# An attention tower on one core: score banks fixed by the parity of the key chunk, a ring of three banks for the row maxima, and more negated maxima written ahead of the scores

## The reference, cut to what matters

```
h = relu(grouped causal conv(emb_table[x]))          # x: (2, 1024) ids, h: (2, 1024, 128), fp32
h = h + Attn(layernorm(h))                           # 8 heads of 64, Wq, Wk, Wv: 512 x 128, Wo: 128 x 512
h = h + FFN(layernorm(h))                            # 8 experts, each on fixed 128-token blocks, exact gelu
Attn(x):  q, k, v = x Wq', x Wk', x Wv'              # per head
          softmax(q k' / 8) v, heads joined, times Wo', plus x
FFN(x):   n = layernorm(x) * ln_g + ln_b;  t = n attn_w' + attn_b + x
          y = fc2(gelu(fc1(t)));  gelu(y next_w' + next_b)
```

## Time and profile before

| what | value |
|---|---|
| median of 3 runs | 402.38 us (402.29 to 402.70) |
| profiled execution, its time | 402.42 us |
| its span in the trace | 400.6 us |
| TensorE clock granted | 0.999 of full speed |
| busy share PE, ACT, DVE, POOL | 97%, 64%, 57%, 73% |

### The profile page before, as it was taken

One profiled execution on the slowest core, in us unless ns is written; L12 is line 12 of the kernel. 1 busy time (PEld: TensorE's weight loads), 2 busy tenths in 40 slices (PEclk: granted clock), 3 DMA queues, 4 the chain that ended last, 5 costly groups with the idle time before them and its releaser, 6 DMA issues.

```text
span 400.6 us, 6437 instructions
## 1 busy us (share of the span) xinstructions
PE 390.3 (97%) x2486; PEld 233.1 (58%) x2486; DVE 227.0 (57%) x310; ACT 254.6 (64%) x347; POOL 292.9 (73%) x145
## 2 busy tenths in 40 slices
PE   8989999999999999999999999999999989999996
PEld 7755554644555455455544644555449445489995
DVE  6998656565666556565656475656562800664322
ACT  3666568586767657666757575767662795436763
POOL 3170399969899899989898999899898588800021
PEclk9999999999999999999999999999999999999999
DMA  4001020101210211132022401240124015000001
GB/s 145 5 0 53 2 53 3 53 2 55 55 53 3 80 29 53 12 97 55 1 54 56 152 8 55 54 157 3 58 52 159 0 56 157 0 2 16 13 28 52
DMA packets 28226, 19.43 MB, mean 49 GB/s; under 512 B 21248, under 2 KB 23680, under 8 KB 28196
## 3 DMA queue, kind: packets, MB, share of 16 engines
q1 hardware_dynamic: 27620, 18.05, 16.7%
q10 hardware_dynamic: 576, 0.98, 0.7%
HBM read 17.72 MB, written 1.17 MB: 47 GB/s over the span
## 4 chain that ended last, share of the span: by engine, by line
PE 91%; DVE 6%; ACT 2%; issue 1%; ACTq 0%
PE acc_o L600 29%; PE slot L588 26%; PE slot L526 10%; PE slot L514 5%; PE slot L535 4%; PE acc_o L656 4%; PE slot L645 4%; PE acc_o L490 2%; PE slot L611 2%; DVE half_maxes L992 1%; PE slot L465 1%; PE slot L551 1%; PE slot L553 1%; PE acc_o L664 1%; PE slot L439 1%; ACT normed L811 1%
## 5 line engine op out<-in xcount | busy, mean ns | idle before, releaser
L992 DVE TENSOR_REDUCE half_maxes<-slot 128x2 f32<-128x1024 f32 x128 | 156.3, 1225 | 96.6 <-PE slot L526 96.4
L778 ACT ACTIVATE probs<-slot 128x1024 f32<-128x1024 f32 x128 | 124.6, 1024 | 82.1 <-PE slot L588 82.1
L600 PE MATMUL acc_o<-probs,v_all 128*64 128x512 f32 x512 | 123.7, 604 | 0.0
L1191 POOL TENSOR_TENSOR sums<-sums,probs 128x1024 f32<-128x1024 f32 x31 | 73.9, 2383 | 2.4 <-ACT probs L778 2.4
L1191 POOL TENSOR_TENSOR odd_sum<-odd_sum,probs 128x1024 f32<-128x1024 f32 x31 | 74.3, 2397 | 0.0
L1191 POOL TENSOR_TENSOR sums<-probs 128x1024 f32<-128x1024 f32 x16 | 37.8, 2365 | 42.6 <-ACT probs L778 42.6
L600 PEld LDWEIGHTS acc_o<-probs,v_all 128*64 128x64 f32 x512 | 31.2, 136 | 58.8 <-issue 39.7
L526 PE MATMUL slot<-k_round,q_round 64*128 64x512 f32 x256 | 56.8, 446 | 1.7 <-DVE half_maxes L992 1.4
L526 PEld LDWEIGHTS slot<-k_round,q_round 64*128 64x128 f32 x256 | 23.6, 183 | 57.2 <-issue 46.3
L588 PE MATMUL slot<-q_round,k_round 64*128 64x512 f32 x256 | 51.6, 399 | 1.1 <-DVE k_rest L987 0.6
L588 PE MATMUL slot<-q_round,k_rest 64*128 64x512 f32 x256 | 50.4, 389 | 0.0
(11 more groups left out here) (124 smaller groups left out, 418.0 us busy)
## 6 DMA issues: line engine op xcount, KB each, us to landing
max_plane<-rows_scratch SPq DMA_DIRECT2D x16, 512.0 KB, 3.7
inv_sb<-inv_scratch SPq DMA_DIRECT2D x14, 256.0 KB, 3.9
max_rows_of<-maxes SPq DMA_DIRECT2D x128, 0.5 KB, 2.0
v_all<-in_fc SPq DMA_DIRECT2D x4, 512.0 KB, 5.7
fc_late<-in_fc SPq DMA_DIRECT2D x4, 512.0 KB, 5.7
out_h<-probs SPq DMA_DIRECT2D x8, 128.0 KB, 1.8
v_all<-in_w ACTq DMA_DIRECT2D x3, 256.0 KB, 3.6
woT<-in_wo SPq DMA_DIRECT2D x1, 256.0 KB, 3.6
```

What stands on the lines that cost most here:

```text
L600: last = pe.matmul(acc_o[head_rows(h), cols], v_all[:, s, kc, head_rows(h)], probs[unit(s, kc, half) % TILES][:, h, :], start=(kc == 0), s ...
L778: act.activation(probs[u % TILES][:, :, :].rearrange("p h n -> p (h n)"), slot[:, :], ACT.Exp, scale=SCALE).then_inc(exped, 1)
L992: dve.reduce_max(half_maxes[:, :, qc, keys], slot[:, :].rearrange("p (h n) -> p h n", h=2), AX.X).then_inc(maxed, 1)
L1191: pool.tensor_tensor(chain[:, :, :], first[:, :, :], probs[kc][:, :, :], ALU.add).then_inc(own, 1)
```

## The change

- **Banks by kind.** A unit with an even `kc`, `k` and `wo` always take banks 0 and 1, one with an odd `kc` and `q` banks 2 and 3. Banks 4, 5, 6 are a ring: each max, `nt` and `xa` takes the next two of it, `den` and `last den` the next one. Bank 7 alone is the output of `pv` for both halves, so the first `pv` of a half waits for the copy `o` of the half before; step 7's half 0 is now copied too. The tail uses a spare ring bank and bank 7 in place of `acc_o`.
- **Waits by bank.** An item waits for the last holder of each of its banks (`holders`). A max in the steps is reduced in two instructions, one for each bank, each of which frees its bank.
- **More filled units.** 96 of 128 are in `FILLED`: 13 of 16 in steps 1 to 6 (not `kc` 0, 1, 3 of half 0), 10 in step 0 and 8 in step 7. Of them 45 (even `kc`, except `kc` 2 of half 0) are halved: item `share`, which stands between the two units of the part before, makes ScalarE write one bank and VectorE the other. The other 51 are written whole by ScalarE behind the second unit.
- **Maxima.** Parts 1 and 2 of step 0 take three each, so all later parts are 14 ahead rather than 12, and step 7 has maxima in part 0 alone.

```diff
-PREFILLED = (2, 4, 6)
-UNFILLED = ((0, 2, 0), (STEPS - 1, 4, 0), (STEPS - 1, 4, 1))
+LATE_PLANES = [(s, kc, 0) for s in range(STEPS) for kc in (0, 1)]
+BEHIND_K, BEHIND_Q = [(s, 2, 0) for s in range(STEPS)], [(s, 3, 0) for s in range(STEPS)]
+UNFILLED = LATE_PLANES + BEHIND_Q + [(0, 2, 0), (0, 0, 1), (0, 1, 1), (STEPS - 1, 2, 0), (STEPS - 1, 4, 0), (STEPS - 1, 5, 0), (STEPS - 1, 0, 1), (STEPS - 1, 1, 1)]
+ALL_UNITS = [(s, kc, half) for s in range(STEPS) for half in range(2) for kc in range(KCH)]
+FILLED = [u for u in ALL_UNITS if u not in UNFILLED]
+HALVED = [u for u in FILLED if u[1] % 2 == 0 and u not in BEHIND_K]
...
+def maxes_before(turn):
+
+    return AHEAD + 2 * turn + min(2, max(0, turn - 1))
...
-    maxes = [("max", *m) for m in MAXES[AHEAD + 2 * (s * PARTS + part):][:2]]
+    turn = s * PARTS + part
+    maxes = [("max", *m) for m in MAXES[maxes_before(turn):maxes_before(turn + 1)]]
     items = maxes[:1]
-    items += [("exp", *u) for u in units_of(s, part)] + maxes[1:]
+    first, second = [("exp", *u) for u in units_of(s, part)]
+    following = units_of(s, part + 1) if part + 1 < PARTS else []
+    items += [first] + [("share", *u) for u in following if u in HALVED] + [second] + maxes[1:]
     beside = beside_values(s, part)
     items += beside
-    if part % 4 < 3:
-        items.append(("fill", *units_of(s, part + 1)[0]))
+    items += [("fill", *u) for u in following if u in FILLED and u not in HALVED]
...
-        items += [("o", s, 0)] * (s + 1 < STEPS) + [("inv", s - 1)] * (s > 0)
+        items += [("o", s, 0)] + [("inv", s - 1)] * (s > 0)
...
+OUT_BANK, EVEN_PAIR, ODD_PAIR, RING = 7, (0, 1), (2, 3), (4, 5, 6)
...
+def step_pairs(items):
+
+    pairs, turn = [], 0
+    for item in items:
+        if item[0] == "exp":
+            pairs.append(ODD_PAIR if item[2] % 2 else EVEN_PAIR)
+        elif item[0] in ("k", "wo"):
+            pairs.append(EVEN_PAIR)
+        elif item[0] == "q":
+            pairs.append(ODD_PAIR)
+        else:
+            count = 1 if item[0] in ("den", "last den") else 2
+            pairs.append(ring_banks(turn, count))
+            turn += count
+    return pairs, turn
...
+def holders(n):
+
+    found = []
+    for bank in PAIRS_OF[n]:
+        held = [m for m in range(n) if bank in PAIRS_OF[m]]
+        if held:
+            found.append((held[-1], PAIRS_OF[held[-1]].index(bank)))
+    return found
...
             def weigh_values(item):
 
                 _, s, kc, half = item
-                cols = slice(half * BANK, (half + 1) * BANK)
                 pe.wait_ge(exped, unit(s, kc, half) + 1)
-                if kc == 0 and s > 0:
-                    pe.wait_ge(o_copied, 2 * s - 1 + half)
+                if kc == 0 and s + half > 0:
+                    pe.wait_ge(o_copied, 2 * s + half)
...
+                        for m, k in holders(n):
+                            pe.wait_ge(*release(ALL_ITEMS[m], k))
```

More of the change, by code:

```diff
@@ L120, in step_items @@
     return items
-NO_SLOT = ("join", "hidden", "pv", "o", "inv", "norms", "fill")
+NO_SLOT = ("join", "hidden", "pv", "o", "inv", "norms", "fill", "share")
 def numbered(items, first):
@@ L141, with ring_banks, filled_up_to @@
 ALL_ITEMS = PROLOGUE + [i for items_of_step in STEP_ITEMS for i in items_of_step if i[0] not in NO_SLOT]
-FIRST_SLOT, LATE_SLOT, SUMS_SLOT = ((FIRST[-1] - 3 + i) % SLOTS for i in range(3))
+OUT_BANK, EVEN_PAIR, ODD_PAIR, RING = 7, (0, 1), (2, 3), (4, 5, 6)
+def ring_banks(start, count):
+    return tuple(RING[(start + i) % len(RING)] for i in range(count))
+def step_pairs(items):
[12 more added lines that the diff above has]
+    return pairs, turn
+STEP_PAIRS, TURN = step_pairs(ALL_ITEMS[len(PROLOGUE):])
+PAIRS_OF = [(2 * (n % SLOTS), 2 * (n % SLOTS) + 1) for n in range(len(PROLOGUE))] + STEP_PAIRS
+SUMS_PAIR, FIRST_PAIR, LATE_PAIR, SPARE_BANK = ring_banks(TURN - 1, 2), EVEN_PAIR, ODD_PAIR, ring_banks(TURN + 1, 1)[0]
+def holders(n):
[5 more added lines that the diff above has]
+    return found
 def unit(s, kc, half):
     return s * UNITS + half * KCH + kc
[L150 to L157, removed]
+def filled_up_to(turn, units):
+    return len([u for u in units if 2 * u[0] + u[2] <= turn])
 def tile_added(s, kc):
@@ L610, in denominators @@
                         quad = 32 * (2 * h + half)
-                        last = pe.matmul(slot[quad:quad + 32, 0:BANK], ones[:, 0:32], sums[s % 2][half][:, h, :], start=True, stop=True)
+                        last = pe.matmul(slot[quad:quad + 32, 0, :], ones[:, 0:32], sums[s % 2][half][:, h, :], start=True, stop=True)
                 last.then_inc(filled, 1)
@@ L623, in last_denominators @@
                     for i, part in enumerate(parts):
-                        last = pe.matmul(slot[head_rows(h), 0:BANK], ones[:, :], part[:, h, :],
+                        last = pe.matmul(slot[head_rows(h), 0, :], ones[:, :], part[:, h, :],
                                          start=(i == 0), stop=(i == len(parts) - 1))
@@ L856, in _ @@
                 for item, n in numbered(STEP_ITEMS[s], FIRST[s]):
-                    if item[0] == "fill" and item[1:] in FILLED:
+                    if item[0] in ("fill", "share") and item[1:] in FILLED:
                         fill(item)
@@ L986, in dve_item @@
                     dve.wait_ge(rounded, 2 * v + (1 if kind == "k" else 2))
-                    dve.tensor_tensor(rest[v % 2][:, :], slot[:, :], whole[v % 2][:, :].bitcast(F32),
-                                      ALU.subtract).then_inc(split, 1)
+                    to, rounded_part = (t[v % 2][:, :].rearrange("p (h n) -> p h n", h=2) for t in (rest, whole))
+                    for halves, source in parts_of(PAIRS_OF[n]):
+                        last = dve.tensor_tensor(to[:, halves, :], source, rounded_part[:, halves, :].bitcast(F32), ALU.subtract)
+                    last.then_inc(split, 1)
                 elif kind == "max":
@@ L1066, in dve_step @@
                         invert(item[1])
+                    elif item[0] == "share" and item[1:] in HALVED:
+                        fill_half(item)
                     elif item[0] == "join":
```

160 lines of the change are left out of this document (102 added, 58 removed).

## The result

| | before | after |
|---|---|---|
| median of 9 runs each | 402.48 us (402.22 to 402.70) | 407.89 us (404.95 to 408.18) |
| ratio | | 1.0108, interval 1.0091 to 1.0124 |
| profiled execution, its span | 402.42, 400.6 us | 404.98, 403.2 us |

The change made the kernel slower; 407.9 lies outside the range, and 400.3 was wrong by 7.6 us. The ratio is that of the mean times (406.87 and 402.46); the medians are 1.3% apart. The executions of the changed kernel come in steps with TensorE's granted clock: three at 404.95 to 405.08 (clock 1.000), one at 406.60 (0.996), five at 407.89 to 408.18 (0.989 to 0.990). The profiled one is of the first kind. So there are two things to explain: 2.5 us at full clock against the kernel before, where 2.1 less was forecast, and 3 us more in five of the nine executions (1.6 in a sixth).

What follows compares the result with a forecast made beforehand. TensorE, busy 390.3 of 400.6 us, was taken as the bound. The terms -10.8 + 4.7 + 2.0 + 2.0 = -2.1, from 402.42, gave 400.3 us, with a range of 396.3 to 405.0.

Steps and rivals of the forecast that it cites:

- Products taken off: TensorE, steps 0 to 6: 47 more filled units each drop a pair of matmuls at 0.23, -10.8 us.
- Hand-overs: Waits between engines in middle parts and step 0, booked at 0.3 us a step, +2.0 us together.
- My first rival: ScalarE becomes the bound: odd unit late in every part with a whole fill behind it, +5.1, 405.4 us; chance 0.20.
- the two ends: Step 0 and step 7, outside the steady state, booked at +4.7 and +2.0 us.
- Step 0: First max +1.1, stalls at third maxima +1.0 and +1.75, two moved maxima +0.85; together +4.7 us.
- The first max: Step 0: it waits for the prologue's last reduction, which still holds banks 4 and 5; +1.1 us.
- Step 7: Serial ScalarE work delays `nt`, normalisations and `xa`; +2.0 us net, with 0 and +4 as ends.
- GpSimd: Rival: GpSimd holds the middle step at 37.7, no gain and the ends stay, 409 us; chance 0.05.
- The shared port: Half fills writing PSUM take no VectorE/GpSimd lock; rival that they do: about 1.0 in 45 parts, some 445 us, chance 0.03.
- the prediction's last sum: Chances by outcome: below 401.6 us 0.60, within 401.6 to 403.2 0.13, slower 0.27, added from own case and rivals.

## Why the prediction was wrong, point by point

- **Products taken off: right.** 64 records of the fourth product where 168 were. The run without the half fills confirms the order of size, net of the waits that they bring: 41 of them back, 6.6 us.
- **Hand-overs, "+2.0, 0.3 a step": the step that failed.** It walked ScalarE "exp 1.23 to 2.26, share to 2.87, exp to 3.80, whole fill to 4.86", with the gaps of 0.03 of the earlier trace rows. They were 0.11 at two places, and the part went from 3.9 to about 4.0. Six steps took 4.0 us more than forecast. The run with the other order of waits gives back 3.5 of them in the same steps and 4.0 in the whole time; the last 0.5 is a step of 36.48 instead of 36.4. I had taken the gap for a property of the engine; it belonged to the two wait lines above the fill, and the diff turned those round. My first rival named the place, and its time, 405.4, is close to the 405.0 at full clock, but with a chance of 0.20 and on a ground other than the order of the waits. Its condition was a delay of over 0.085 for each of 5 units a step. Measured, ScalarE lost 0.16 a part, and TensorE 0.12 for each of the 5 (37.07 less 36.48). That its time came so close is in part luck: it had 5.1 us of delay where 4.0 were measured, and the 0.6 that makes up most of the difference came from the two ends.
- **The clock: not foreseen.** I had put two waits of about 1.5 us into part 5 of step 7 and priced them as waits only. In 7 of 15 executions of the changed kernel they cost 3 us again through the granted clock, and in 2 more 1.6. This is the rest of the error: 405.0 to 407.9, as five of the first nine were at the upper level. The Trainium skill, "TensorE: Matmul & The Clock Gate", section "Part 1: The HAM clock gate", says that TensorE's clock falls to half behind idleness, and that the same kernel shows another number of slow matmuls from run to run. The window at 0.50 and the three levels agree, and the run with seven matmuls in the waits is the test.
- **Step 0: right.** +2.75 forecast, +2.7 measured from `k` to `k`; the third maxima waited 0.91 and 1.62 (1.0 and 1.75). The first max cost 1.3 (1.1), and the run with other banks for it gave 0.9 back.
- **Step 7: right.** +2.0 forecast, +2.4 measured; `nt` at 326.48 (326.15), `xa` at 337.70 (337.2).
- **GpSimd: right.** It idles 0.62 and more at each half of the middle steps of after, and 0.35 and 0.61 where a step takes 36.48: not the bound.
- **The shared port: right.** VectorE's half fill at 199.13 took 0.69 beside a GpSimd sum that still took 2.38. The rule of "VectorE: DVE Perf Modes" in the Trainium skill, section "Why PSUM operands drop a tier", keeps an operation with an operand in PSUM out of the mode that uses both ports, and on this the prediction rested. The trace agrees: all 45 half fills ran beside a sum and took 685 to 696 ns.

The gain went here, at full clock: 52 products, -12.0; first max +1.3; step 0, above all its third maxima and their stalls, +3.9; hand-overs in six steps +5.8; step 7 +3.5; sum +2.5, as measured. (Each is the measured stage plus its products at 0.23.) Of the 5.8, 3.5 are the order and number of the waits.

Two chances of the prediction's last sum are off by 0.01: 0.05 and 0.07 make 0.12, and 0.20, 0.05 and 0.03 make 0.28. Its other sums come out.

## What to carry to other kernels

When a change moves a wait in a queue that has little slack, read the gap in front of that instruction as the cost of its waits in their order, not of the engine: put the wait that is met last first, and name each condition once. Price a stall of TensorE twice, as a stall and as the clock behind it, where two follow each other closely: 1.50 and about 1 us, 2 us apart, did it in 14 of 33 executions here, while the kernel before has single waits of 0.93 and 1.11 in step 7 and none of its 41 executions fell. Read a lost wait in the weight loads (PEld) too, since the matmuls' busy time hid it. Where a steady state is won by giving another engine more work, leave the work out in the stages where that engine is already the bound: 8 fills fewer in step 7 were 2.35 us faster.

## What the runs showed of the hardware

- An ACTIVATE that depends on the ACTIVATE just ahead of it on ScalarE started 0.03 us behind it when that wait stood first and a wait already met stood behind it; 0.09 with the order turned round, in two different kernels; 0.11 with the same condition waited for twice. In the middle steps this held for every such fill. Why the order matters inside the engine no run here shows, nor whether VectorE or GpSimd do the same.
- An ACTIVATE that does not depend on the one ahead starts before that one's end. In the run with banks and waits alone, where the fill follows the other unit's exp, two exps from 201.83 end at 203.78 and the fill starts at 203.67, 0.11 earlier. So the dependence itself costs 0.14 us even with the best order.
- The engine that was signalled across (VectorE, 199.13, its wait for the exp first) started earlier than the engine that waited for itself (ScalarE, 199.21, its wait for the exp last and twice).
- Two waits of TensorE of 1.50 and 0.84 us were followed by a granted clock of 0.50 in one execution, while the same kernel ran six others at 400.86 to 401.53; 1.50 and 0.97 by 0.60 and 0.55 in another kernel. Seven 128-wide matmuls in such waits kept it at full speed in five of five.
